# Feed-forward layer norm: the variance from one product with a matrix of 1/128, roots on ScalarE, the scaling on GpSimd

## The reference

```python
def ffn_layer(x, g, bln, W1, b1, W2, b2):
    mu = x.mean(-1, keepdims=True)
    var = ((x - mu) ** 2).mean(-1, keepdims=True)
    xn = (x - mu) / jnp.sqrt(var + 1e-05) * g + bln
    hg = xn @ W1 + b1
    a, gate = jnp.split(hg, 2, -1)
    return a * jax.nn.gelu(gate, approximate=False) @ W2 + b2
for i in range(6):
    x = attn_layer(shift_tokens(x), Wqkv[i], q_scale[i], k_scale[i], Wo[i]) + x
    x = ffn_layer(shift_tokens(x), ln_g[i], ln_b[i], W1[i], b1[i], W2[i], b2[i]) + x
```

## Time and profile before

| | us |
|---|---|
| three runs | 1635.75, 1634.16, 1635.62; median 1635.62 |
| the profiled execution: its own time | 1636.74 |
| its span, first to last instruction | 1634.9 |
| TensorE busy | 1595.9 (98% of the span) |
| VectorE / ScalarE / GpSimd busy | 1395.7 / 1341.3 / 1321.6 (85%, 82%, 81%) |
| granted TensorE clock, mean over the span | 0.994 |

### The profile page before, as it was taken

One profiled execution on the slowest core, in us unless ns is written; L12 is line 12 of the kernel. 1 busy time (PEld: TensorE's weight loads), 2 busy tenths in 40 slices (PEclk: granted clock), 3 DMA queues, 4 the chain that ended last, 5 costly groups with the idle time before them and its releaser, 6 DMA issues.

```text
span 1634.9 us, 50862 instructions
## 1 busy us (share of the span) xinstructions
PE 1595.9 (98%) x19920; PEld 1370.2 (84%) x19920; DVE 1395.7 (85%) x2021; ACT 1341.3 (82%) x2516; POOL 1321.6 (81%) x1278
## 2 busy tenths in 40 slices
PE   5999999999999999999999999999999999999997
PEld 3778888888888888888888888888888888888886
DVE  7888888888888888888888888888888899999975
ACT  5778888888888888888888888888888888888874
POOL 9888899888889888889888889888888777777741
PEclk8999999999999999999999999999999999999999
DMA  5234233333323344232344324244332332222231
GB/s 166 80 114 138 73 95 93 113 109 100 106 75 93 102 117 121 75 108 70 96 112 127 99 73 111 70 121 109 110 95 76 85 101 73 78 73 70 64 90 58
DMA packets 184872, 156.89 MB, mean 96 GB/s; under 512 B 111551, under 2 KB 156093, under 8 KB 184637
## 3 DMA queue, kind: packets, MB, share of 16 engines
q1 hardware_dynamic: 184636, 153.64, 33.6%
HBM read 27.56 MB, written 1.05 MB: 17 GB/s over the span
## 4 chain that ended last, share of the span: by engine, by line
PE 87%; ACT 4%; POOL 2%; DVE 2%; issue 2%; DMA 0%; SPq 0%; ACTq 0%; POOLq 0%; DVEq 0%
PE ps_pv L807 12%; PE ps_s L783 11%; PE ps_pv L826 10%; PE ps_tr L744 9%; PE ps_qn L719 9%; PE ps_qn L720 7%; PE ps_qn L721 7%; PE ps_tr L731 5%; PE ps_pv L816 3%; PE ps_qn L906 2%; PE ps_qn L907 2%; PE ps_s L766 2%; PE ps_qn L908 2%; PE ps_qn L893 1%; PE ps_pv L864 1%
## 5 line engine op out<-in xcount | busy, mean ns | idle before, releaser
L2032 POOL TENSOR_TENSOR qk<-qk,t 128x1024 f32<-128x1024 f32 x192 | 456.0, 2376 | 82.0 <-DVE qk L1550 81.4
L1547 DVE TENSOR_TENSOR t<-ps_qn,tab 128x512 f32<-128x512 f32 x384 | 264.3, 688 | 121.5 <-ACT sq L1145 109.9
L2044 POOL TENSOR_TENSOR qkr<-qk,rinv 128x1024 f32<-128x1024 f32 x192 | 361.5, 1903 | 8.0 <-POOL rinv L2024 0.8
L1132 ACT ACTIVATE pbd<-ps_tr 64x512 f32<-64x512 f32 x384 | 226.4, 590 | 55.3 <-PE ps_tr L731 51.7
L719 PE MATMUL ps_qn<-w_hi,xs_hi 128*128 128x512 f32 x576 | 260.9, 453 | 10.8 <-DVE qk L1550 8.1
L1550 DVE TENSOR_TENSOR qk<-ps_qn,tab 128x512 f32<-128x512 f32 x384 | 260.9, 679 | 0.0
L1145 ACT ACTIVATE sq<-ps_qn 128x512 f32<-128x512 f32 x384 | 228.8, 596 | 32.7 <-PE ps_qn L721 27.9
L1178 ACT ACTIVATE qbd<-ps_tr 64x512 f32<-64x512 f32 x384 | 227.3, 592 | 34.2 <-PE ps_tr L744 28.7
L720 PE MATMUL ps_qn<-w_lo,xs_hi 128*128 128x512 f32 x576 | 229.8, 399 | 0.0
L721 PE MATMUL ps_qn<-w_hi,xs_lo 128*128 128x512 f32 x576 | 229.2, 398 | 0.0
L1560 DVE TENSOR_REDUCE ss<-sq 128x32 f32<-128x2048 f32 x96 | 216.5, 2256 | 0.0
(11 more groups left out here) (177 smaller groups left out, 3178.7 us busy)
## 6 DMA issues: line engine op xcount, KB each, us to landing
v_own<-v_new SPq DMA_DIRECT2D x96, 512.0 KB, 3.3
v_back<-v_new SPq DMA_DIRECT2D x96, 384.0 KB, 3.5
v_back<-v_own SPq DMA_DIRECT2D x94, 128.0 KB, 2.3
kT<-kT SPq DMA_DIRECT2D x84, 128.0 KB, 2.7
w_raw<-in_Wqkv SPq DMA_DIRECT2D x18, 512.0 KB, 5.0
rot<-in_rot SPq DMA_DIRECT2D x48, 128.0 KB, 2.7
fx<-xmid SPq DMA_DIRECT2D x96, 64.0 KB, 2.1
xsh<-x SPq DMA_DIRECT2D x190, 32.0 KB, 2.6
```

Of the source, the lines that this page charges most:

```text
L1547: v.tensor_tensor(t2[:, part].rearrange("p (h s d) -> p h s d", s=2, d=DH // 2), swapped, tab[:, 2 * k + 1:2 * k + 2, :].rearrange("p o (s ...
L2032: g.tensor_tensor(qk[b][:, part], qk[b][:, part], t2[:, part], ALU.add).then_inc(added[b], 1)
L2044: g.tensor_tensor(qkr[b][:, part].rearrange("p (h d) -> p h d", d=DH), qk[b][:, part].rearrange("p (h d) -> p h d", d=DH), rinv[b][:, k * ...
```

## The change

The variance is no longer formed on the tokens' partitions and sent back. In `b=1` one matmul with a 128x128 matrix of 1/128 (`mean_w`) as stationary operand and `fsq` as moving operand gives the variance of each token on all partitions; it takes the place of the product with `ones`, and the two one-column matmuls in `b=0` go. ScalarE forms the root from PSUM in two instructions over 256 columns (`inverse_deviation`: Ln with epsilon as a bias column, Exp with scale -0.5) at the end of `b=1`, behind the switch of its tables and ahead of everything of the next half. GpSimd multiplies `fc` by it in the next `b=0` (`scale_centred`), between its two additions of the rotation; the diagonal goes. The gain moves into the two offset activations as a scale column. VectorE loses the epsilon addition and its own scaling; its residual addition of `("out", 1)` now waits for the Ln (`var_logged`), since it frees the bank. The copy of the next centred values (`centre_copy`) waits for GpSimd's scaling. The head norms' chain is down to 32 columns. In the drain the path by two matmuls, a power and a diagonal is kept for the last three tiles.

```diff
-                    if b == 0 and valid(n):
-                        last = variance(i, bank)
...
-                def ffn_broadcast(i):
-                    n = i - 3
-                    if not valid(n):
-                        return
-                    bank, k = fill(pv_order, i, spread_of(i))
-                    if i.n >= STEPS:
-                        ring_free(pe, pv_done, bank, k)
-                    pe.wait_ge(diag_ready, n.n + 1)
+                def ffn_variance(i):
+
+                    if not valid(i - 3):
+                        return
+                    bank, k = fill(pv_order, i, ("out", 1))
+
+                    wait_fill(pe, qn_done, qn_order, i, "centre")
+                    mm(ps_pv[bank][:, DOWN], mean_w[:, :], flat(fsq), start=True, stop=True).then_inc(pv_full[bank], 1)
...
+                def inverse_deviation(i):
+                    n = i - 3
+                    if not valid(n):
+                        return
+                    after_first(act, fxn_scaled, n.n, n)
+                    wait_fill(act, pv_full, pv_order, i, variance_of(i))
+                    bank, k = fill(pv_order, i, variance_of(i))
+                    root = ln_root[:, :, :].rearrange("p b t -> p (b t)")
+                    f(root, ps_pv[bank][:, DOWN], ACT.Ln, bias=eps_col[:, :]).then_inc(var_logged, 1)
+                    act.wait_ge(var_logged, n.n + 1)
+                    f(root, root, ACT.Exp, scale=-0.5).then_inc(ln_rooted, 1)
+
+                def scaled(i):
+
+                    if i.n > STEPS:
+                        wait_fill(act, pv_done, pv_order, i - 1, "spread")
+                    else:
+                        act.wait_ge(fxn_scaled, (i - 4).n + 1)
...
-                    wait_fill(act, pv_done, pv_order, i - 1, spread_of(i - 1))
+                    scaled(i)
                     act.wait_ge(gb_in, (m.layer + 1) * 16)
-                    f(fxn_hi[:, :, :], fxn[:, :, :], ACT.Identity, bias=ln_gb[:, SM_B:SM_B + 1], scale=1.0).then_inc(fxn_high, 1)
+                    f(fxn_hi[:, :, :], fxn[:, :, :], ACT.Identity, bias=ln_gb[:, SM_B:SM_B + 1],
+                      scale=ln_gb[:, SM_G:SM_G + 1]).then_inc(fxn_high, 1)
...
-                        wait_fill(act, pv_done, pv_order, i - 1, spread_of(i - 1))
+                        scaled(i)
...
                         nc.scalar.preload_act_table_set("natural_log_exp_and_others")
+                    if b == 1:
+                        inverse_deviation(i)
...
-                def scale_centred(bank, m):
-                    dve.wait_ge(gb_in, (m.layer + 1) * 16)
-                    return v.scalar_tensor_tensor(fxn[:, :, :].rearrange("p b t -> p (b t)"), ps_pv[bank][:, DOWN],
-                                                  ln_gb[:, SM_G:SM_G + 1], fc[:, :, :].rearrange("p b t -> p (b t)"),
-                                                  ALU.mult, ALU.mult)
...
-                    if valid(n):
-                        if not n.first:
-                            dve.wait_ge(newton[0], NEWTON * i.n)
-                        last = v.tensor_scalar(ss[0][:, 2 * HEADS:], ps_pv[bank][:, VAR:VAR + B], LN_EPS, None, ALU.add)
...
-                    if valid(j):
-                        last = residual(bank, j, 1)
                     if valid(m):
-                        wait_fill(dve, qn_full, qn_order, i, ("up", 2))
-                        last = scale_centred(bank, m)
-                    last.then_inc(pv_done[bank], 1)
+
+                        dve.wait_ge(var_logged, m.n + 1)
+                    residual(bank, j, 1).then_inc(pv_done[bank], 1)
...
+                def scale_centred(i):
+                    m = i - 4
+                    if not valid(m):
+                        return
+                    pool.wait_ge(ln_rooted, m.n + 1)
+
+                    wait_fill(pool, qn_full, qn_order, i - 1, ("up", 2))
+                    g.tensor_tensor(fxn[:, :, :], fc[:, :, :], ln_root[:, :, :], ALU.mult).then_inc(fxn_scaled, 1)
...
                     add(i, b, 0)
-                    if b == 1:
-                        spread_roots(i)
+                    if b == 0:
+                        scale_centred(i)
                     rec_gated(i, b)
...
+                    scale_centred(END)
```

More of the change, by code:

```diff
@@ L184, in variance_of @@
 def variance_of(i):
-    return "variance" if i.n >= STEPS else ("out", 0)
-def spread_of(i):
-    return "spread" if i.n >= STEPS else ("out", 1)
+    return "variance" if i.n >= STEPS else ("out", 1)
 def down_of(i):
@@ L266, in layer_tiles @@
     w.ones = sb("ones", [P, P])
+    w.mean_w = sb("mean_w", [P, P])
     w.v_own = per_stream("v_own", [P, INNER])
@@ L361, in per_stream @@
             return [sb(f"{name}{b}", shape) for b in range(B)]
-        w_hi, w_lo, wo, w1, w1_hi, w1_lo, w2, ln_gb, b2, b1, rot, scales, centre_w, mean_col, ones, v_own, v_back, qbd, kT, pbd = (
-            w.w_hi, w.w_lo, w.wo, w.w1, w.w1_hi, w.w1_lo, w.w2, w.ln_gb, w.b2, w.b1, w.rot, w.scales, w.centre_w, w.mean_col, w.ones,
+        w_hi, w_lo, wo, w1, w1_hi, w1_lo, w2, ln_gb, b2, b1, rot, scales, centre_w, mean_col, mean_w, ones, v_own, v_back, qbd, kT, pbd = (
+            w.w_hi, w.w_lo, w.wo, w.w1, w.w1_hi, w.w1_lo, w.w2, w.ln_gb, w.b2, w.b1, w.rot, w.scales, w.centre_w, w.mean_col, w.mean_w, w.ones,
             w.v_own, w.v_back, w.qbd, w.kT, w.pbd)
@@ L381, in layers @@
         oT = sb("oT", [P, HP, 2, 2 * WINDOW])
-        fc, fsq, fxn, diag = (sb(n, [P, B, P]) for n in ("fc", "fsq", "fxn", "diag"))
+        fc, fsq, fxn, ln_root = (sb(n, [P, B, P]) for n in ("fc", "fsq", "fxn", "ln_root"))
+        diag = ln_root
         fxn_hi, fxn_lo = (sb(n, [P, B, P], F32R) for n in ("fxn_hi", "fxn_lo"))
@@ L495, in norm_tile @@
             return (i, 0) if b else (i - 1, 1)
-        def root_span(s, b, n):
-            return 0 if valid(s) else 2 * HEADS, 2 * HEADS + B if b == 0 and valid(n) else 2 * HEADS
+        NORMS = slice(0, 2 * HEADS)
         def early(t, b):
@@ L1054, in drain @@
                     mask(END, 1)
-                    ffn_broadcast(END)
+                    last_broadcast(END)
                     scores(END, 1, 0)
@@ L1186, in exps, with inverse_root @@
                     f(pr[b][:, :, :, :], pr[b][:, :, :, :], ACT.Exp, scale=QK_SCALE).then_inc(exp_ready[b], 1)
-                def inverse_root(s, b, n):
-                    lo, hi = root_span(s, b, n)
-                    if lo == hi:
+                def inverse_root(s, b):
+                    if not valid(s):
                         return
                     act.wait_ge(newton[b], NEWTON * s.n + 1)
-                    f(lnv[:, lo:hi], floored[:, lo:hi], ACT.Ln).then_inc(logged[b], 1)
+                    f(lnv[:, NORMS], floored[:, NORMS], ACT.Ln).then_inc(logged[b], 1)
                     act.wait_ge(logged[b], s.n + 1)
-                    if hi > 2 * HEADS:
-                        after_first(act, diag_ready, n.n, n)
-                    f(rinv[b][:, lo:hi], lnv[:, lo:hi], ACT.Exp, scale=-0.5).then_inc(rooted[b], 1)
+                    f(rinv[b][:, NORMS], lnv[:, NORMS], ACT.Exp, scale=-0.5).then_inc(rooted[b], 1)
+                def inverse_deviation(i):
[14 more added lines that the diff above has]
+                        act.wait_ge(fxn_scaled, (i - 4).n + 1)
                 def round_fxn(i):
@@ L1371, in half @@
                     new_layer = i.t == TILES - 1 and b == 1 and not i.last_layer
-                    inverse_root(*norm_tile(i, b), i - 3)
+                    inverse_root(*norm_tile(i, b))
                     evac_probs(i, b, 0)
@@ L1463, in drain @@
                 def drain():
-                    inverse_root(END - 1, 1, END - 3)
+                    inverse_root(END - 1, 1)
                     evac_probs(END, 0, 0)
@@ L2062, in low_fxn, with last_spread @@
                     g.tensor_tensor(fxn_lo[:, :, :], fxn[:, :, :], fxn_hi[:, :, :].bitcast(F32), ALU.subtract).then_inc(fxn_ready, 1)
-                def spread(i):
-                    if not (i - 3).first:
-                        wait_fill(pool, pv_full, pv_order, i - 1, spread_of(i - 1))
+                def scale_centred(i):
[5 more added lines that the diff above has]
+                    g.tensor_tensor(fxn[:, :, :], fc[:, :, :], ln_root[:, :, :], ALU.mult).then_inc(fxn_scaled, 1)
+                def last_spread(i):
+                    pool.wait_ge(var_root, i.n - STEPS + 1)
+                    if i.n > STEPS:
+                        wait_fill(pool, pv_full, pv_order, i - 1, "spread")
                     g.tensor_tensor(diag[:, :, :], ident[:, :].unsqueeze(1).broadcast_to([P, B, P]),
@@ L2105, in half @@
                     new_layer = i.t == TILES - 1 and b == 1 and not i.last_layer
-                    newton_step(s, other, i - 3)
+                    newton_step(s, other)
                     scale(s, other, 1)
@@ L2153, in clear @@
                     g.memset(ones[:, :], 1.0)
+                    g.memset(mean_w[:, :], 1.0 / DIM)
```

58 lines of the change are left out of this document (26 added, 32 removed).

## The result

| | before | changed |
|---|---|---|
| median of 19 runs each, us | 1635.37 (1633.71 to 1636.11) | 1638.17 (1636.52 to 1640.15) |
| profiled execution, us | 1636.74 | 1638.73 |
| its span, us | 1634.9 | 1636.9 |
| mean granted TensorE clock | 0.994 | 0.995 |

The ratio is 1.0019 with a 95% interval of 1.0012 to 1.0026: 2.8 us slower. I had forecast 1639.0 us, from 1635.6 us before: 3.4 us slower.

What follows compares the result with a forecast made beforehand. TensorE's queue, and who hands it operands late, bounds the kernel. Terms -16.7 + 14.5 + 1.5 + 3.0 + 0.4 + 0.7 = +3.4 us give a median of 1639.0 us, range 1630 to 1646.

Steps and rivals of the forecast that it cites:

- The two matmuls: TensorE in b=0: dropping the one-column matmuls saves 0.37 us in each of 45 steps, -16.7 us.
- The pair: ScalarE's Ln and Exp at the b=1 to b=0 seam take 0.82 us, pbd 0.34 late: +14.5 us over 44 seams.
- 0.97 us of step for one of lateness: At the seam, lateness of pbd lengthens TensorE's step at 0.97 to one, read from a change of layer.
- VectorE: Its residual waits for the Ln, but its own scaling goes, so rmax comes no later: 0.
- GpSimd in ordinary steps: GpSimd's new scaling in b=0 takes 0.787 us and delays nobody in ordinary steps: 0.
- the cover: Spare time around GpSimd's scaling in b=0: 0.3 us before its second addition and 0.3 before ScalarE's copy of fc.
- +0.4 us in all, for the columns alone: ScalarE's gain scale columns, 0.2 us a step, may show in tiles where it rounds W1 or a value weight: +0.4.
- At a change of layer: Five times: later pbd +1.5 us; fc copy 1.5 late, qbd 1.2 late, 0.6 reaching TensorE, +3.0 (2.5 to 6).
- The sign of steps of 33.3 to 33.7 at a change of layer: Sign that the forecast is right: ScalarE's fc copy waits for GpSimd at layer changes, with steps of 33.3 to 33.7.
- The rule of the Trainium skill that I had set aside: Noted under the late-scaling rival: no row separates it, and VectorE's instructions at this place read PSUM.
- Drain and start: One more GpSimd scaling in the drain, 0 to 1.0, and a starting memset, 0 to 0.2: +0.7 us.
- The rival of a scaling late in every step: GpSimd's scaling ends over 0.3 us later than computed, delaying TensorE in all 44 steps: about 1652; 9 in 100.

Runs made afterwards that it cites:

- experiment 2: Kernel before without the two one-column variance matmuls in b=0, VectorE's epsilon addition reading a constant instead: 1618.62 us, ratio 0.9902.
- 1: Kernel before with an unused Ln and Exp over 256 columns added on ScalarE behind the second table load: 1651.75 us, ratio 1.0106.
- 4: Changed kernel with a third 256-column operation (an Exp of fsq) on ScalarE behind the Ln and Exp at the seam: 1651.63 us, ratio 1.0104.
- experiment 3: Changed kernel with the Exp moved from the seam to behind ScalarE's fourth square in the next b=0, Ln left in place: 1625.89 us, ratio 0.9944.
- 8: Changed kernel with GpSimd's scaling done twice in each b=0: 1653.14 us, ratio 1.0107.
- 5: Changed kernel with scale=1.0 instead of the gain column in both offset activations: 1635.65 us, ratio 1.0005.
- 11: Changed kernel, Exp behind fourth square, scaling before first addition in each layer's first tile, VectorE's recurrence product behind the value copies: 1620.47 us, ratio 0.9911.
- 9: Changed kernel with GpSimd's scaling cut to one column per stream and constant 0.5 as the offset activations' scale: 1632.51 us, ratio 0.9983.
- 10: Changed kernel with VectorE's 128x384 recurrence product moved, in b=0, from ahead of the sum of squares to behind the value copies: 1634.49 us, ratio 0.9999.

## Why the prediction was right, and where not

*What bounds the kernel.* TensorE's queue, and who hands it operands late. This held: in a plain step taking two matmuls out gives their time back in full (experiment 2), and delaying `pbd` costs it (1, 4).

*The two matmuls.* Forecast were 0.37 us a step and 16.7 in all; found were 0.41 in a plain step and 16.0 in all. Right in kind and size.

*The pair.* It takes 0.83 us against 0.82, `pbd` is 0.34 us late as worked out, and a step costs 0.31 us against 0.33. I had forecast 0.97 us of step for one of lateness; 0.91 was found over the first 0.34 us and 1.0 beyond (3, 4). My estimate of 0.83 us, worked out from the Trainium skill's figures ("ScalarE: Activation LUTs", section "What ACT_TABLE_LOAD costs"), agrees with the trace for the pair.

*VectorE.* 0 was right: the residual waits 0.22 us and the step is none the longer for it (3).

*GpSimd in ordinary steps.* 0 was right where no weights are rounded, and the cover was about what I said: 0.40 us at `fc`, 0.28 behind it. Doubling shows it (8): it holds for 0.7 us more of GpSimd, but not where ScalarE also rounds weights. The forecast treated that case as +0.4 us in all, for the columns alone. Six ordinary steps of the changed kernel are 0.1 to 0.5 us above 31.61, together 1.5 us, where the kernel before had 0.3 above its 31.71; 0.9 us of it go with the columns (5).

*At a change of layer.* `fc` waits 1.54 us, 1.5 forecast; the seam steps are 1.3 us longer, 1.3 by the forecast's terms. The steps behind are 1.0 us longer each (0.7 in the last of the four) instead of 0.6. `qbd` was as late as I had said: it starts 0.85 us later behind the centring than before, and the transposes come 0.37 earlier, which is 1.2. What was mis-sized is how much of that TensorE's six products hide. I took half, 0.6 of 1.2; they hid only 0.1, and 1.1 us came through. My own upper bound was that nothing is hidden. The sign of steps of 33.3 to 33.7 at a change of layer did not come: I had put both costs into one step, and they fall into two, of 32.65 and 32.71.

*The recurrence steps.* Here the step failed that said "0 in ordinary steps" for GpSimd and meant all 44. I expected them 0.04 us shorter. Five of the eight are 0.12 to 0.14 longer, the one with W1's rounding 0.94, the first 0.11 shorter, together +1.5 us. In such a step taking the two matmuls out gives 0.45 (2), the pair takes 0.30 (3), and GpSimd's scaling takes 0.29 (38.07 in experiment 3 against 37.78 in experiment 2) through VectorE's product. With the Exp moved away, moving the product gives 0.30 back (11); in the changed kernel either remedy gives 0.41 to 0.42 (9, 10), so there the costs overlap in part. In the step with W1's rounding moving the product gives 1.05 back (10), more than the whole loss. The rule of the Trainium skill that I had set aside ("GPSIMD Engine Reference", section "1. Specifications": GpSimd shares SBUF interfaces with VectorE, contended by a VectorE instruction with two SBUF inputs) is what these rows look like. I had looked for such an instruction at the seam alone, and there was none.

*Drain and start.* Forecast +0.7; the one pair of profiles shows -3.1, but kernels that leave both untouched differ there as much (below), so this term stays open.

So the total was within 0.8 us partly by luck. By parts of the span, with -0.37 for the one product gone from the start, my terms were -0.7 for the ordinary steps (-1.5 found), +1.3 for the seams (+1.3), +2.8 behind them (+3.8), -0.3 beside the recurrence (+1.5), and +0.3 for start and drain (-3.1). The 44 steps between start and drain came out 2 us dearer than I had them, and an unexplained difference at both ends covered that. The rival of a scaling late in every step (1652) did not come true. Experiment 8 reaches its number (1653), but with plain steps still at 31.61.

## What to carry to other kernels

Before you add work to an engine off the path, lay its queue beside the instruction that the bounding engine waits for, and put the new work into an idle gap of that queue, not where its input happens to be ready: the same Exp cost 12 us at the seam, and seven microseconds later nothing in an ordinary step. Follow a new instruction down its own engine's queue to the next value that somebody waits for, and do that once in each kind of step (here layer changes, weight roundings and the recurrence), since a cover that holds in most steps can be gone in the others. If a second way lies behind the first, clearing the first shows it, and the gain is only the difference of the two. A change whose parts cancel to 0.2% can hold a gain of 1%: take each part alone before judging it.

## What the runs showed of the hardware

A VectorE instruction with both inputs in SBUF (scalar_tensor_tensor, 128x384, fp32) takes 0.54 to 0.55 us where no long GpSimd instruction is under way (10, 11). Started while GpSimd is in a 1.90 us tensor_tensor, it ended 0.41 to 0.42 us behind GpSimd's end in each of the eleven kernels that have it there, and so took 0.78 to 2.16 us, by when it began. VectorE's neighbours with a PSUM input or one SBUF operand show no such stretch: `ss` takes 2.27 us either way, the products of `rotate` 0.68 to 0.69. GpSimd pays too, one instruction later: its subtraction of 128x128 (`xs_lo`), which starts when the long instruction ends and VectorE's product is still under way, takes 0.77 to 0.80 us there, where its median elsewhere is 0.46 (0.45 at the same place in experiment 10).

Parts that the edits hardly touch differ from one profile to another. From the last centring beside a full step to the next, in the drain, it took 23.8 to 27.1 us over these kernels, in most with a wait for a transfer at its end (1.84 us of wait before, when it took 27.06; 0.37 us in the changed kernel, 25.53). Up to the second centring it took 124.7 to 126.9 us, with a mean granted TensorE clock of 0.83 to 0.97 in the first 50 us. Differences below 3 us between two profiled spans say nothing by themselves; the lengths of like steps agree within some 0.03 us in nearly all cases.
